# Four of ten attention units transposed by DMA instead of TensorE, with scores computed seven units ahead

## The reference

```
latents = x @ W_down.T                      # 64 values a token, shared by all heads
q = x @ W_q.T;  keys = latents @ W_uk.T;  values = latents @ W_uv.T
scores = q . k / sqrt(128), causal;  attn = softmax(scores)
out = (attn @ values) @ W_o.T
```

## Time and profile before

| | us |
|---|---|
| median of 3 runs | 253.59 (251.93 to 253.77) |
| the profiled execution, its own time | 253.38 |
| its span in the profile | 251.4 |
| PE busy in the span | 238.5 |
| DVE busy | 205.1 |
| ACT busy | 163.5 |
| POOL busy | 71.8 |

### The profile page before, as it was taken

One profiled execution on the slowest core, in us unless ns is written; L12 is line 12 of the kernel. 1 busy time (PEld: TensorE's weight loads), 2 busy tenths in 40 slices (PEclk: granted clock), 3 DMA queues, 4 the chain that ended last, 5 costly groups with the idle time before them and its releaser, 6 DMA issues.

```text
span 251.4 us, 7272 instructions
## 1 busy us (share of the span) xinstructions
PE 238.5 (95%) x2643; PEld 182.6 (73%) x2668; DVE 205.1 (82%) x487; ACT 163.5 (65%) x320; POOL 71.8 (29%) x127
## 2 busy tenths in 40 slices
PE   7599999999889999999999999999999899999995
PEld 2545469975667868888788787887888688955474
DVE  2848779996869999989999999999999508268793
ACT  2626473395777888879889798888798500335560
POOL 8320055000002435433444335253454000210230
PEclk9979999999999999999999999999999999999999
DMA  6999300001102103316024141250426130000004
GB/s 218 241 317 365 65 3 1 3 0 42 44 0 53 37 12 83 73 42 125 0 74 93 41 104 22 61 107 21 95 51 86 23 63 3 0 0 3 0 1 167
DMA packets 34792, 17.21 MB, mean 68 GB/s; under 512 B 25484, under 2 KB 34520, under 8 KB 34520
## 3 DMA queue, kind: packets, MB, share of 16 engines
q1 hardware_dynamic: 33576, 15.81, 26.8%
...
...
## 4 chain that ended last, share of the span: by engine, by line
PE 79%; DVE 12%; DMA 3%; issue 2%; ACT 1%; SPq 1%; DVEq 0%
PE bank L880 12%; PE bank L1081 12%; PE bank L852 9%; PE bank L1156 8%; PE bank L1072 7%; PE bank L987 6%; PE bank L1071 4%; PE bank L1095 3%; DMA cT<-in_L_ffn_w_dram 3%; PE bank L1094 3%; PE bank L1096 3%; PE bank L1028 3%; DVE pT_lo L756 2%; PE bank L1073 2%; DVE nmax L751 2%
## 5 line engine op out<-in xcount | busy, mean ns | idle before, releaser
L506 ACT ACTIVATE prob<-bank,nmax 128x384 f32<-128x384 f32 (+3 forms) x128 | 62.3, 527 | 8.2 <-DVE nmax L747 6.8
L756 DVE TENSOR_TENSOR pT_lo<-bank,pT_hi 128x512 f16<-128x512 f32 x80 | 54.5, 682 | 3.1 <-ACT pT_hi L512 2.4
L512 ACT CAST pT_hi<-bank 128x512 f16<-128x512 f32 x80 | 46.7, 584 | 11.0 <-PE bank L1081 10.6
L1081 PE MATMUL bank<-ident,prob 128*128 128x128 f32 x320 | 50.5, 280 | 0.6 <-ACT prob L506 0.6
L387 POOL TENSOR_TENSOR cst<-craw,rsum 128x256 f32<-128x256 f32 x30 | 18.4, 612 | 93.2 <-DVE craw L765 93.2
L1094 PE MATMUL bank<-lat,pT_hi 128*128 128x65 bf16 x320 | 37.7, 193 | 2.3 <-DVE pT_lo L756 2.3
L1095 PE MATMUL bank<-lat,pT_hi 128*128 128x64 bf16 x320 | 37.8, 195 | 0.0
L1072 PE MATMUL bank<-latT_lo,wqo 128*128 128x384 bf16 (+3 forms) x128 | 36.6, 299 | 1.2
L1096 PE MATMUL bank<-lat,pT_lo 128*128 128x65 bf16 x320 | 37.5, 192 | 0.0
L1094 PEld LDWEIGHTS bank<-lat,pT_hi 128*128 128x128 f16 x320 | 30.1, 96 | 7.2 <-DVE pT_lo L756 2.0
L747 DVE TENSOR_REDUCE nmax<-bank 128x1 f32<-128x512 f32 (+1 forms) x48 | 32.6, 681 | 1.9 <-PE bank L1073 1.9
...
## 6 DMA issues: line engine op xcount, KB each, us to landing
...
cT<-in_L_attn_W_uk_dram SPq DMA_DIRECT2D x1, 512.0 KB, 10.8
...
```

The lines of the kernel that those rows point to most:

```text
L506: last = nc.scalar.activation(prob[:, u % 2, cols], bank[SCORE_BANK[u]][:, cols], ACT.Exp, bias=nmax[:, u, n:n + 1])
L512: nc.scalar.copy(pT_hi[:, j % 2, :], bank[3 + j % 2][:, :]).then_inc(pThi_ready, 1)
L756: nc.vector.tensor_tensor(pT_lo[:, j % 2, :], bank[3 + j % 2][:, :], pT_hi[:, j % 2, :], ALU.subtract).then_inc(pTlo_ready, 1)
L1081: last = nc.tensor.transpose(bank[3 + j % 2][:, blk(k)], prob[:, j % 2, blk(k)], ident[:, :])
```

## The change

- `BY_DMA` = units 1, 3, 6, 8 of each pair are no longer transposed by PE. ACT (`high_part`) and POOL (`low_part`) split their fp32 probabilities into `prob_hl`, SP turns both halves with one DMA transpose of 128x1024 fp16 into `turned` (`turn_probabilities`), and PE's `context` reads that. Both tiles have two places. `high_part(j)` waits until the DMA of the second last such unit has landed (`prob_turned`), and the DMA waits until that unit's context has been read (`turned_used`).
- The other six (`BY_PE`) are transposed by PE two of their own kind ahead (`second_next`), from a ring `prob` of five.
- In step j, PE does scores(j+7), context(j), transposes. Before step 0, seven scores are written rather than four.
- Queries are made two pairs ahead, in steps 5 and 7 and at the end of the step; those of pair 1 are made before the first scores. SP moves both halves of a pair's queries at once, by 4 DMAs twice as long (8 before). The last loop turn has none, so that pairs 6 and 7 are both without queries.
- The context of a pair is turned by one DMA transpose of 128x2048 instead of two of 128x1024, one pair later in SP's order (its two parts now lie side by side in `wide`).

```diff
-    SCORE_BANK = [0, 1, 7, 2, 0, 1, 2, 0, 1, 7]
-    HELD_BY = [-3, -2, -1, -4, 0, 1, 3, 4, 5, None]
+    SCORE_BANK = [7, 0, 1, 2, 0, 1, 2, 0, 1, 2]
+    HELD_BY = [None, -3, -2, -1, 1, 2, 3, 4, 5, 6]
+    LEAD = 7
+    BY_DMA = [1, 3, 6, 8]
+    BY_PE = [u for u in range(UNITS) if u not in BY_DMA]
+    ND, NPE = len(BY_DMA), len(BY_PE)
+    PROBS = 5
...
+        wide = sb("wide", [P, 2, 4 * T], F32)
+        ffn_buf = wide[:, 0, :].rearrange("p (a n) -> p a n", a=4)
-        woT_buf = sb("woT_buf", [P, 2, H * D], BF16)
+        woT_buf = wide[:, 1, :].bitcast(BF16).rearrange("p (a n) -> p a n", a=2)
-        prob = sb("prob", [P, 2, SEQ], F32)
+        prob = sb("prob", [P, PROBS, SEQ], F32)
+        prob_hl = sb("prob_hl", [P, 2, 2, SEQ], FP16)
+        turned = sb("turned", [P, 2, 2, SEQ], FP16)
...
+        def second_next(j):
+
+            n = BY_PE.index(j % UNITS) + 2
+            return j - j % UNITS + n // NPE * UNITS + BY_PE[n % NPE]
...
+            def move_queries(i):
+                sp.wait_ge(u_lo, i * 2 + 2)
+                for side in range(2):
+                    for part in range(2):
+                        sp.dma_start(uc[LAT * part:LAT * (part + 1), i * 2 + side:i * 2 + side + 1, :],
+                                     stage[LAT * side:LAT * (side + 1), part:part + 1, :]).then_inc(u_moved, 16)
+
+            def turn_probabilities(i, j):
+                d = in_order(BY_DMA, i, j)
+                sp.wait_ge(prob_lo, d + 1)
+                if d >= 2:
+                    sp.wait_ge(turned_used, d - 1)
+                sp.dma_start_transpose(turned[:, d % 2, :, :].rearrange("p a (k q) -> p (a k) q", k=SB),
+                                       prob_hl[:, d % 2, :, :].rearrange("p a n -> p (a n)")).then_inc(prob_turned[d % 2], 16)
+
+            for i in range(2):
+                move_queries(i)
+            for j in BY_DMA[:2]:
+                turn_probabilities(0, j)
             for i in range(NP):
-                for t in range(2):
-                    sp.wait_ge(u_lo, i * 2 + (t + 1))
-                    for side in range(2):
-                        for part in range(2):
-                            sp.dma_start(uc[LAT * part:LAT * (part + 1), i * 2 + side:i * 2 + side + 1, tokens(t)],
-                                         stage[LAT * side:LAT * (side + 1), part:part + 1, tokens(t)]).then_inc(u_moved[t], 16)
-                if i >= 2:
-                    sp.wait_ge(clo_ready, B + 2 * B * (i - 1))
-                    transpose_context(i - 2, 0, NB, cT_early)
-            sp.wait_ge(clo_ready, B + 2 * B * (NP - 1))
-            transpose_context(NP - 2, 0, NB, cT_mid)
+                turn_probabilities(i, 6)
+                turn_probabilities(i, 8)
+                if i > 0:
+                    sp.wait_ge(clo_ready, B + 2 * B * i)
+                    sp.dma_start_transpose(cT[:, i - 1, :, :, :].rearrange("p a n t -> p (a n) t"),
+                                           c_hl[:, i - 1, :, :, :].rearrange("p a n c -> p (a n c)")).then_inc(cT_mid if i == NP - 1 else cT_early, 16)
+                if i < NP - 1:
+                    turn_probabilities(i + 1, 1)
+                if i < NP - 2:
+                    move_queries(i + 2)
+                if i < NP - 1:
+                    turn_probabilities(i + 1, 3)
             for b in range(B):
                 sp.wait_ge(clo_ready, B + 2 * B * (NP - 1) + b + 1)
                 sp.wait_ge(clo_last, b + 1)
-                transpose_context(NP - 1, SB * b, SB * (b + 1), cT_last[b])
+                transpose_last_context(b)
...
+            def low_part(i, j):
+                d = in_order(BY_DMA, i, j)
+                r = BY_DMA.index(j % UNITS) % 2
+                pool.wait_ge(prob_hi, d + 1)
+                if not (isinstance(i, int) and i == 0 and j in BY_DMA[:2]):
+                    pool.wait_ge(prob_turned[r], i * (8 * ND) + 16 * ((j // UNITS * ND + BY_DMA.index(j % UNITS)) // 2))
+                nc.gpsimd.tensor_tensor(prob_hl[:, r, 1, :], prob[:, j % PROBS, :], prob_hl[:, r, 0, :],
+                                        ALU.subtract).then_inc(prob_lo, 1)
+
+            for j in (1, 3, 6):
+                low_part(0, j)
             with pool.Fori(0, NP - 1) as i:
-                for side in range(2):
-                    divide_context(i, side)
-            divide_context(NP - 1, 0)
+                low_part(i, 8)
+                divide_context(i, 0, 0)
+                low_part(i, UNITS + 1)
+                divide_context(i, 0, 1)
+                low_part(i, UNITS + 3)
+                divide_context(i, 1, 0)
+                low_part(i, UNITS + 6)
+                divide_context(i, 1, 1)
+            low_part(NP - 1, 8)
+            for b in range(B):
+                divide_context(NP - 1, 0, b)
...
                 act.wait_ge(max_ready, i * UNITS + (j + 1))
+                if (u - PROBS) % UNITS in BY_DMA and not (isinstance(i, int) and i == 0 and j < PROBS):
+                    act.wait_ge(prob_lo, in_order(BY_DMA, i, j - PROBS) + 1)
                 for n, (b, q, at) in enumerate(HEAD_UNITS[u % HU]):
                     cols = slice(at, at + P * (q + 1))
-                    last = nc.scalar.activation(prob[:, u % 2, cols], bank[SCORE_BANK[u]][:, cols], ACT.Exp,
+                    last = nc.scalar.activation(prob[:, u % PROBS, cols], bank[SCORE_BANK[u]][:, cols], ACT.Exp,
                                                 bias=nmax[:, u, n:n + 1])
                 last.then_inc(prob_ready, 1)
 
+            def high_part(i, j):
+                d = BY_DMA.index(j % UNITS)
+                act.wait_ge(prob_ready, i * UNITS + (j + 1))
+                if not (isinstance(i, int) and i == 0 and j in BY_DMA[:2]):
+                    act.wait_ge(prob_turned[d % 2], i * (8 * ND) + 16 * ((j // UNITS * ND + d) // 2))
+                nc.scalar.copy(prob_hl[:, d % 2, 0, :], prob[:, j % PROBS, :]).then_inc(prob_hi, 1)
...
             def attention_step(i, j, queries=True):
-                if not beyond(i, j + 3):
-                    exponent(i, j + 3)
-                if queries and j in (1, 3):
-                    split_queries(i + 1, j // 2)
-                if not beyond(i, j + 2):
-                    split(i, j + 2)
+                if not beyond(i, j + LEAD - 1):
+                    exponent(i, j + LEAD - 1)
+                    if (j + LEAD - 1) % UNITS in BY_DMA:
+                        high_part(i, j + LEAD - 1)
+                if queries and j in (5, 7):
+                    split_queries(i + 2, (j - 5) // 2)
+                if j % UNITS in BY_PE and not beyond(i, second_next(j)):
+                    split(i, second_next(j))
...
-            exponent(0, 0)
-            exponent(0, 1)
-            split(0, 0)
-            exponent(0, 2)
-            split(0, 1)
-            attention_step(0, 0)
-            with act.Fori(0, NP - 1) as i:
-                for j in range(1, UNITS + 1):
+            for t in range(2):
+                split_queries(1, t)
+            for j in range(LEAD - 1):
+                exponent(0, j)
+                if j in BY_DMA:
+                    high_part(0, j)
+                if j in BY_PE[:2]:
+                    split(0, j)
+            for j in range(5):
+                attention_step(0, j)
+            with act.Fori(0, NP - 2) as i:
+                for j in range(5, 5 + UNITS):
                     attention_step(i, j)
-            for j in range(1, UNITS - 2):
+            for j in range(5, 5 + UNITS):
+                attention_step(NP - 2, j, queries=False)
...
                     take_context(i, side, LAST_UNIT.index(unit))
-                if not beyond(i, j + 1):
-                    split(i, j + 1)
-                if not beyond(i, j + 4):
-                    row_max(i, j + 4)
-                if queries and j in (1, 3):
-                    split_queries(i + 1, j // 2)
+                if j > 0 and (j - 1) % UNITS in BY_PE and not beyond(i, second_next(j - 1)):
+                    split(i, second_next(j - 1))
+                if not beyond(i, j + LEAD):
+                    row_max(i, j + LEAD)
+                if queries and j in (5, 7):
+                    split_queries(i + 2, (j - 5) // 2)
...
             def queries(i, t):
 
-                if not (isinstance(i, int) and t == 0):
+                if not (isinstance(i, int) and i == 0 and t == 0):
                     pe.wait_ge(u_lo, i * 2 + t)
+                if not isinstance(i, int) and t == 0:
+                    pe.wait_ge(prob_ready, i * UNITS - UNITS + 1)
...
             def transposes(i, j):
+                n = in_order(BY_PE, i, j)
+                r = BY_PE.index(j % UNITS) % 2
                 pe.wait_ge(prob_ready, i * UNITS + (j + 1))
-                if not (isinstance(i, int) and i == 0 and j < 2):
-                    pe.wait_ge(pTlo_ready, i * UNITS + (j - 1))
+                if not (isinstance(i, int) and n < 2):
+                    pe.wait_ge(pTlo_ready, n - 1)
```

(48 more changed lines are left out.)

98 lines of the change are left out of this document (56 added, 42 removed).

## The result

The changed kernel takes 267.93 us (median of 4 runs, 266.84 to 270.06); the kernel before, run beside it, 252.76 (4 runs, 251.86 to 253.77). The ratio is 1.0615, with a 95% interval of 1.0569 to 1.0661. A ratio here counts only those runs of a kernel that lie within 1.5% of its fastest. The kernel is slower by 6%, where the prediction had 258.0 and a range up to 262.5: the sign was right, the size was not. The forecast of "slower" rested on the start (5.1 us), with a pair at 16.1 us against 16.20; most of the 6% comes from the pair, so the sign came out right in part by luck.

What follows compares the result with a forecast made beforehand. The prediction took a chain through SP's queue, 16.1 us a pair, as the bound. With the start (5.1), six chain turns and the end, span 251.4 + 4.6 = 256.0, plus 1.98 around it: 258.0 us, range 248.5 to 262.5.

Steps and rivals of the forecast that it cites:

- the start: Before the first scores: pair 1's queries come first, first exponentials at about 73.5 instead of 68.41, cost 5.1 us, not hidden.
- What bounds the kernel before, and what leaves PE: In a pair: PE sets the pace at 16.2 us; four transposes of 0.47 leave it, so PE alone needs 14.3.
- The price of SP's items: SP's queue: a move holds it 0.6 us, a turn lands after 3.3, the double context transpose after 4.6.
- The failed step: In the loop: a chain through SP's queue, from one turn's landing to the next, takes 16.1 us a pair.
- the real ring: Found by measurement: hand-overs between ACT and DVE, returning one pair later to the same instruction, 17.62 us, without PE or DMA.
- Not saved later: After the start: what its steps do is not saved later where PE isn't the bound; start cost 5.1 us.
- The end: Last two pairs, without queries: 20.4 us after the chain's 182.3, so attention ends at 202.7 instead of 198.10.
- A longer chain: Rival, SP's queue: moves of 0.79 or a landing of 4.1 add 0.8 a pair each; 262.8 or more, chance 0.17.
- A shorter chain: Rival: without ACT and DVE backlog only PE and SP are in the ring, 15.05 us a pair; 251.7, chance 0.22.
- PE stays the bound: Rival, in the loop: waits for the landing are short, a pair takes 14.3 us; 246.3 in all, chance 0.16.
- What would show it: Signs in the changed profile: two DMA waits, PE about 14.2 a pair, transposes 192, turn behind moves, first exponentials near 73.5.
- The two waits for a DMA once a pair: PE's context of unit 3 waits for `turned`, ACT's cast to `prob_hl` of unit 8 for a DMA, 1 us or more.

Runs made afterwards that it cites:

- the second experiment: In the changed kernel, SP issues the turn of unit 3 ahead of the four moves of queries instead of behind them; 270.03 us in one run.
- the last experiment: Changed kernel with DVE's maxima before its split, pair 1's queries behind first scores, and DVE's loop subtraction of queries one step later; 253.26 us, ratio 1.0016.

## Why the prediction was wrong

- **What bounds the kernel before, and what leaves PE: right.** PE in a pair of the experiment with the maxima first works for 14.46 us (14.3 predicted), DVE 12.9 to 13.2 (13.0), ACT 13.54 (14.0), POOL 11.2 (11.4).
- **The price of SP's items: near.** A move twice as long holds the queue 0.598 us (0.6 taken), the double context transpose lands in 4.4 (4.6), a turn in 2.8 where 3.3 was taken from the earlier trace rows. The view of the turns in the changed kernel (min/median/max):

```profile
L335 SPq DMA_TRANSPOSE turned<-prob_hl x32: 1232/1233/1743, 77.4 to 208.2; - x32
...
DMA to landing us min/median/max: 2.8/2.8/4.4
```

- **The failed step: that the landing of the turn is what ACT waits for, and that the list from there is the longest ring.** The prediction began its count at a landing and followed the engines only until SP's issue, "SP four moves 2.4; turn of 23: 3.3. Sum 15.8". Behind ACT's second cast of queries, 129.28 in the rows above, and DVE's subtraction of them, 129.89, it left the engines for SP. The engines went on: DVE took a context, then split 20 at 130.90, maxima of 25, exponentials 25 at 132.28. The turn issued behind the moves at 115.48 had landed 2.8 us later, at 118.3, and ACT came to that high part only at 120.14, 1.9 us too late to notice. All pieces of the real ring stand in the prediction's own list (DVE's maxima "stand behind its split"), but it was never closed without the DMA. Closed at the prediction's own prices, from the high part of 18 to that of 28, it is 8.8 us as listed up to high part 23, 2.9 for the second half of the queries, a context taken (0.40, from the trace), split 20 and maxima 25, 5.3 for exponentials 25 to 28, and eight hand-overs of 0.03: 17.3 us, by this estimate longer than the 16.1 that were named as the pace. Measured, the miss is 17.62 - 16.1 = 1.5 us a pair, 9.1 us for six pairs.
- **The check that was missing:** the idle sums. With 16.1 us a pair the prediction left ACT 2.1 us idle and DVE 3.1, and named the DMA as what they wait for; it did not ask which of the two would wait for the other.
- **The start: right in kind, a little high.** First exponentials at 72.64 (73.5), so +4.2 of 5.1. Two errors partly cancel: the cast of pair 1's first half began at 66.72 where 68.07 was taken, and from there it took 5.9 us instead of 5.4. "Not saved later" was half right: 2 of these 4.2 us are the order's cost by the two runs with the queries behind, the rest returns in the ramp.
- **The end.** 202.7 predicted, less 0.9 for the start, plus 9.1 for the ring, is 210.9; it was 211.76. The tail was right within 0.9 us.
- **The range.** It was said to take in moves or landings at their upper bound and to leave out about 2 in 10, but the longer chain is priced at 262.8 or more with either of them and the range ends at 262.5, so by these prices it left out that rival (0.17) besides most of the first (0.16).
- **The rivals.** "A longer chain" ended nearest (262.8 or more), with a reason that the second experiment refutes. "A shorter chain" is not the pace of the changed kernel, but it is that of the last experiment, 15.35 us where it said 15.05. "PE stays the bound" is nearly what the kernel does once two lines are swapped: 14.84 a pair and 249 us, where the rival said 14.3 and 246.3. Its price was near, and so was the saving of PE; the order on DVE hid both.
- **What would show it.** PE's transposes, the place of the turn behind the moves and the start came as listed, PE's busy time in a pair at 14.95 instead of 14.2. The two waits for a DMA once a pair were missing (PE's matmuls wait for `turned` twice, 1.3 us in all, and never in the loop), and that had been named as the sign of being wrong.
